# A three-stage decoder block on one core: the prologue's projections as three fp32r products, with context and inputs laid out ahead and loads on two queues

## The reference, cut to what matters

```python
# x: (2, 256, 128), ctx: (2, 512, 128), everything float32
x = x + attn(layernorm(x))          # 16 heads of 64, softmax over queries
x = x + xattn(layernorm(x), ctx)    # 16 heads of 8, 512 keys, mask over keys
x = x + moe(layernorm(x))           # 8 experts, 2 chosen, and a shared one; all 9 computed
# attn:  q, k, v = x_hat @ Wq + bq, x_hat @ Wk + bk, x_hat @ Wv + bv      (128 x 1024 each)
#        prob = softmax(k q^T / 8, axis=-2);  out = concat(prob @ v) @ Wo + bo
# xattn: q from x_hat, k and v from ctx (128 x 128 weights)
```

## Time and profile before

| | us |
|---|---|
| median of 3 runs | 220.93 |
| lowest and highest | 220.23, 222.34 |
| span of the profiled execution | 219.2 |
| TensorE busy | 202.3 (92%) |
| mean granted TensorE clock | 0.984 |

### The profile page before, as it was taken

One profiled execution on the slowest core, in us unless ns is written; L12 is line 12 of the kernel. 1 busy time (PEld: TensorE's weight loads), 2 busy tenths in 40 slices (PEclk: granted clock), 3 DMA queues, 4 the chain that ended last, 5 costly groups with the idle time before them and its releaser, 6 DMA issues.

```text
span 219.2 us, 4318 instructions
## 1 busy us (share of the span) xinstructions
PE 202.3 (92%) x1536; PEld 147.0 (67%) x1536; DVE 163.7 (75%) x424; ACT 126.4 (58%) x297; POOL 90.6 (41%) x136
## 2 busy tenths in 40 slices
PE   7599999799999799699796999999898999999993
PEld 7346466576767467456463665666565899999993
DVE  2628657878687799567999999998995685548843
ACT  2325436767575485536694989989696532372220
POOL 1989703764747466400899930000120002711332
PEclk9979999999999999979999999999999999999999
DMA  5960735999552003300601500000000000000000
GB/s 156 376 176 0 191 48 67 138 111 137 82 151 94 0 0 89 59 0 14 204 1 36 111 0 0 3 1 3 1 0 3 0 3 1 3 0 24 3 0 24
DMA packets 11740, 12.67 MB, mean 58 GB/s; under 512 B 848, under 2 KB 10064, under 8 KB 11648
## 3 DMA queue, kind: packets, MB, share of 16 engines
q1 hardware_dynamic: 11480, 12.20, 25.8%
q0 software_dynamic: 96, 0.20, 0.4%
q10 hardware_dynamic: 144, 0.01, 0.1%
HBM read 10.96 MB, written 1.44 MB: 57 GB/s over the span
## 4 chain that ended last, share of the span: by engine, by line
PE 74%; DVE 14%; issue 4%; ACT 3%; POOL 2%; DMA 2%; POOLq 0%; DVEq 0%
PE ps L830 12%; PE ps L792 8%; PE ps L721 7%; PE ps L736 7%; PE ps L851 7%; PE ps L629 7%; PE ps L708 6%; PE ps L770 6%; PE ps L752 5%; PE ps L641 4%; DVE q_t L1040 3%; DVE x_hat L915 2%; DMA x_in<-in_x 2%; PE ps L808 1%; DVE prob_t L1113 1%
## 5 line engine op out<-in xcount | busy, mean ns | idle before, releaser
L446 POOL TENSOR_TENSOR prob<-prob,rec 128x512 f32<-128x512 f32 x32 | 32.6, 1041 | 29.6 <-DVE rec L1095 29.6
L1040 DVE CUSTOM_DVE_ANT_0 q_t<-ps,mask_add 128x512 f32<-128x512 f32 x64 | 41.3, 682 | 2.1 <-PE ps L752 2.1
L531 ACT ACTIVATE prob<-ps,low 128x256 f32<-128x256 f32 x64 | 29.5, 475 | 18.4 <-DVE low L1030 18.4
L556 ACT ACTIVATE q_t<-q_t,low 128x512 f32<-128x512 f32 x44 | 29.4, 719 | 10.4 <-DVE low L1040 10.4
L386 POOL TENSOR_SCALAR var_eps<-mean_var 128x2 f32<-128x2 f32 (+1 forms) x5 | 1.1, 226 | 68.3 <-DVE mean_var L907 68.3
L792 PE MATMUL ps<-ident,q_t 128*128 128x128 f32 x176 | 23.4, 275 | 3.9 <-DVE place_o L1113 2.0
L792 PEld LDWEIGHTS ps<-ident,q_t 128*128 128x128 f32 x176 | 19.9, 141 | 9.2 <-issue 4.5
L1030 DVE TENSOR_REDUCE low<-ps 128x2 f32<-128x512 f32 x32 | 20.5, 683 | 6.3 <-PE ps L708 6.2
L1110 DVE COPY prob_t<-ps 128x512 f32<-128x512 f32 x32 | 20.6, 683 | 2.8 <-PE ps L736 2.8
L541 ACT ACTIVATE q_t<-ps 128x512 f32<-128x512 f32 x18 | 10.6, 598 | 21.0 <-PE ps L830 21.0
L752 PE MATMUL ps<-k_stack,q_stack 72*128 72x512 bf16 x64 | 19.3, 386 | 1.6 <-issue 1.6
(11 more groups left out here) (167 smaller groups left out, 422.3 us busy)
## 6 DMA issues: line engine op xcount, KB each, us to landing
k_stack<-k_dram SPq DMA_DIRECT2D x9, 256.0 KB
q_stack<-q_dram SPq DMA_DIRECT2D x6, 192.0 KB
wg<-in_L_ffn_w_gate SPq DMA_DIRECT2D x1, 1024.0 KB, 20.3
wu<-in_L_ffn_w_up SPq DMA_DIRECT2D x1, 1024.0 KB, 27.9
k_dram<-prob SPq DMA_DIRECT2D x1, 768.0 KB, 3.6
prob_t<-in_ctx SPq DMA_DIRECT2D x2, 256.0 KB, 4.0
w_in<-in_L_attn_Wq SPq DMA_DIRECT2D x1, 512.0 KB, 6.3
w_in<-in_L_attn_Wk SPq DMA_DIRECT2D x1, 512.0 KB, 7.1
```

The costliest lines, as they stand in the source:

```text
L446: nc.gpsimd.tensor_tensor(pr, pr, rec1[:, s % 2, r, :].unsqueeze(2).to_broadcast([P, C, S]), ALU.mult).then_inc(s_norm1, 1)
L531: e = nc.scalar.activation(prob1[:, s % 3, r, c * S:(c + 1) * S], ps[:, 2 * (s % 2) + r, c * S:(c + 1) * S], ACT.Exp, bias=low1[:, s % 2, ...
L556: nc.scalar.activation(prob2[n % 3][:, c, :], score2[n % 2][:, c, :], ACT.Exp, bias=low2[:, n % 2, c:c + 1], scale=-1.0).then_inc(s_exp2, 1)
L1040: nc.vector.tensor_tensor_reduce(out=score2[n % 2][:, c, :], in0=ps[:, 2 * (n % 2) + c, :], in1=mask_add[:, c, :], scale=1.0, scalar=3e38, ...
```

## The change

Five things change, all in the prologue:

1. `q` and `k` items are three fp32r products each instead of one fp32 product. The parts of the weights are made in halves of 512 columns: ACT rounds (`high_weights`), DVE subtracts (`low_weights`), both into the new tile `qk_parts`. The parts of `x_hat_t` (`xv_parts`) come straight from the PSUM bank of `x_t`: ACT rounds, DVE subtracts. POOL's split of `x_hat_t` and DVE's copy are gone.
2. The context comes transposed from the host, and x with a partition's four token rows side by side. The items `ctx_t` are gone, with their two ACT copies. The new order of items is `kx` 0, `kx` 1, `x_t`, `vx` 0, `vx` 1, then all `q` and `k`.
3. `wq1` and `wk1` are loaded in four halves (256 KB each) on ACT's queue, beside SP's.
4. POOL clears `v2` and fills `rank` before `reciprocal_std` instead of behind it.
5. The split of `k2_t` moves from DVE to POOL, in front of `x_bo`; its parts lie in another place of the tile `prob1`, so that ACT's wait for their way to DRAM (`d_kdram`) stands in front of the second head of `exp1(1)` instead of ahead of the whole loop.

```diff
 def items():
-    out = [("ctx_t", 0, "act"), ("ctx_t", 1, "act"), ("kx", 0, "act"), ("x_t", 0, "dve"), ("kx", 1, "act")]
+    out = [("kx", 0, "act"), ("kx", 1, "act"), ("x_t", 0, "dve"), ("vx", 0, "act"), ("vx", 1, "act")]
     for p in range(NP):
-        if p == 2:
-            out += [("vx", 0, "act"), ("vx", 1, "act")]
         out += [("q", p, "act"), ("k", p, "dve")]
...
+        qk_parts = retired("qk_parts", [P, 2, 2, H1 * HD1], F32R)
...
-            load(x_in[:, :, :], chunks(a["x"]), d_x)
-            for b in range(B):
-                load(ctx_in[:, b * KC:(b + 1) * KC, :], chunks(a["ctx_1024"])[:, b * KC:(b + 1) * KC, :], d_ctx[b])
+            load(x_in[:, :, :], a["x"], d_x)
+            load(ctx_t, a["ctx_1024"], d_ctx)
             load(wk2[:, :], a["L0_xattn_Wk"], d_wk2)
-            load(wq1, a["L0_attn_Wq"], d_wq1)
-            load(wk1, a["L0_attn_Wk"], d_wk1)
...
-            reciprocal_std(0, 0, NC_)
             nc.gpsimd.memset(v2[:, :, :, HD2 + 1:CW], 0.0)
...
+            reciprocal_std(0, 0, NC_)
...
             split(wv1, [wv1_parts[:, i, :] for i in range(2)]).then_inc(s_vparts, 1)
-            pool.wait_ge(s_ev["dve"], evacuated(index_of("x_t", 0))[1])
-            split(x_hat_t[:, :], [xv_parts[:, i, :] for i in range(2)]).then_inc(s_vparts, 1)
+            pool.wait_ge(s_ev["act"], evacuated(index_of("kx", 1))[1])
+            link(nc.gpsimd.tensor_copy(k2_parts[:, 0, :], k2_t))
+            link(nc.gpsimd.tensor_tensor(k2_rest, k2_t, k2_parts[:, 0, :], ALU.subtract))
+            link(nc.gpsimd.tensor_copy(k2_parts[:, 1, :], k2_rest))
+            nc.gpsimd.tensor_tensor(k2_parts[:, 2, :], k2_rest, k2_parts[:, 1, :], ALU.subtract).then_inc(s_kparts, 1)
...
+            for half in range(2):
+                for i, w in enumerate((wq1, wk1)):
+                    cols = slice(half * BANK, (half + 1) * BANK)
+                    act.dma_start(w[:, cols], a["L0_attn_W" + "qk"[i]][:, cols]).then_inc(d_qk[i][half], 16)
...
+            def high_weights(half):
+                cols = slice(half * BANK, (half + 1) * BANK)
+                for i, w in enumerate((wq1, wk1)):
+                    act.wait_ge(d_qk[i][half], 16)
+                    nc.scalar.copy(qk_parts[:, i, 0, cols], w[:, cols]).then_inc(s_whi, 1)
+
             for j, (kind, which, engine) in enumerate(ITEMS):
+                if (kind, which) == ("kx", 0):
+                    high_weights(0)
+                elif kind == "x_t":
+                    act.wait_ge(s_item, j + 1)
+                    nc.scalar.copy(xv_parts[:, 0, :], ps[:, j % 8, :]).then_inc(s_xhi, 1)
+                    high_weights(1)
                 if engine == "act":
                     evacuate(j, kind, which)
...
-            act.wait_ge(d_kdram, 16)
...
+                    if s == 1 and r == 1:
+                        act.wait_ge(d_kdram, 16)
...
-                    w = wq1 if kind == "q" else wk1
-                    last = mm(bank, w[:, which * P:(which + 1) * P], x_hat_t[:, :], start=True, stop=True)
+                    for part, (xi, wi) in enumerate(BIG_PARTS):
+                        last = mm(bank, qk_parts[:, i, wi, which * P:(which + 1) * P], xv_parts[:, xi, :],
+                                  start=part == 0, stop=part == len(BIG_PARTS) - 1)
...
+            def low_weights(half):
+                cols = slice(half * BANK, (half + 1) * BANK)
+                for i, w in enumerate((wq1, wk1)):
+                    dve.wait_ge(s_whi, 2 * half + i + 1)
+                    nc.vector.tensor_tensor(qk_parts[:, i, 1, cols], w[:, cols], qk_parts[:, i, 0, cols].bitcast(F32),
+                                            ALU.subtract).then_inc(s_qkparts, 1)
+
+            low_weights(0)
...
-                    ins = nc.vector.tensor_copy(x_hat_t[:, :], bank)
+                    dve.wait_ge(s_xhi, 1)
+                    ins = nc.vector.tensor_tensor(xv_parts[:, 1, :], bank, xv_parts[:, 0, :].bitcast(F32), ALU.subtract)
...
-                if (kind, which) == ("k", 1):
-                    dve.wait_ge(s_ev["act"], evacuated(index_of("kx", 1))[1])
-                    split(k2_t, k2_rest, k2_parts).then_inc(s_kparts, 1)
+                if kind == "x_t":
+                    low_weights(1)
...
+    laid["x"] = np.asarray(inputs["x"]).reshape(NC_, P, D).transpose(1, 0, 2)
+    laid["ctx_1024"] = np.asarray(inputs["ctx_1024"]).reshape(TK, D).T
```

More of the change, by code:

```diff
@@ L210, in build @@
         prob1_t_flat = prob1_t[:, :, :, :].rearrange("p a r n -> p (a r n)")
-        k2_parts = prob1_flat[:, 0:PARTS * TK // 2].bitcast(BF16).rearrange("p (j t) -> p j t", j=PARTS)
+        k2_parts = prob1_flat[:, PARTS * TK // 2:PARTS * TK].bitcast(BF16).rearrange("p (j t) -> p j t", j=PARTS)
         mask_in = prob1_t_flat[:, 0:C * SK].bitcast(mybir.dt.int32).rearrange("p (c k) -> p c k", c=C)
-        ctx_in = prob1_t_flat[:, C * SK:C * SK + B * KC * D].rearrange("p (c d) -> p c d", d=D)
         context = retired("context", [P, 3, TK])
@@ L280, in build @@
         d_x, d_wk2, d_wv2, d_wq2 = map(sem, ("d_x", "d_wk2", "d_wv2", "d_wq2"))
-        d_ctx = [sem(f"d_ctx{b}") for b in range(B)]
-        d_wq1, d_wk1, d_wv1, d_wo1 = map(sem, ("d_wq1", "d_wk1", "d_wv1", "d_wo1"))
+        d_ctx, d_wv1, d_wo1 = map(sem, ("d_ctx", "d_wv1", "d_wo1"))
+        d_qk = [[sem(f"d_w{n}1_{half}") for half in range(2)] for n in "qk"]
         d_bias, d_mask, d_bo, d_wo2, d_ffn, d_wd = map(sem, ("d_bias", "d_mask", "d_bo", "d_wo2", "d_ffn", "d_wd"))
@@ L293, in build @@
         s_ev = {"act": sem("s_ev_act"), "dve": sem("s_ev_dve")}
-        s_bq = sem("s_bq")
+        s_bq, s_whi, s_qkparts, s_xhi = map(sem, ("s_bq", "s_whi", "s_qkparts", "s_xhi"))
         s_var, s_rstd, s_xhat, s_xhat_ps, s_xhat_t = map(sem, ("s_var", "s_rstd", "s_xhat", "s_xhat_ps", "s_xhat_t"))
@@ L484, in evacuate @@
                 bank = ps[:, j % 8, :]
-                if kind == "ctx_t":
-                    ins = nc.scalar.copy(ctx_t[:, which * BANK:(which + 1) * BANK], bank)
-                elif kind == "kx":
+                if kind == "kx":
                     ins = nc.scalar.activation(k2_t[:, which * BANK:(which + 1) * BANK], bank, ACT.Identity,
@@ L603, in _ @@
                     pe.wait_ge(s_ev[engine], value)
[L604 to L608, removed]
+                if kind == "kx":
                     if which == 0:
                         pe.wait_ge(d_wk2, 16)
-                        pe.wait_ge(s_ev["act"], 2)
+                        pe.wait_ge(d_ctx, 16)
                     last = mm(bank, wk2[:, :], ctx_t[:, which * BANK:(which + 1) * BANK], start=True, stop=True)
@@ L623, in _ @@
                 else:
-                    if which == 0:
-                        pe.wait_ge(d_wq1 if kind == "q" else d_wk1, 16)
+                    i = "qk".index(kind)
+                    if which % (NP // 2) == 0:
+                        pe.wait_ge(s_qkparts, 2 * (which // (NP // 2)) + i + 1)
                     if kind == "q" and which == 0:
                         pe.wait_ge(s_ev["dve"], evacuated(index_of("x_t", 0))[1])
-                    w = wq1 if kind == "q" else wk1
-                    last = mm(bank, w[:, which * P:(which + 1) * P], x_hat_t[:, :], start=True, stop=True)
+                    for part, (xi, wi) in enumerate(BIG_PARTS):
+                        last = mm(bank, qk_parts[:, i, wi, which * P:(which + 1) * P], xv_parts[:, xi, :],
+                                  start=part == 0, stop=part == len(BIG_PARTS) - 1)
                 last.then_inc(s_item, 1)
@@ L705, in scores1 @@
                         pe.wait_ge(s_exp1, 2 * (s - 2) + r + 1)
+                    else:
+                        engine, value = evacuated(max(j for j in range(len(ITEMS)) if j % 8 == 2 * s + r))
+                        pe.wait_ge(s_ev[engine], value)
                     rows = slice(HD1 * r, HD1 * (r + 1))
@@ L800, in values_of_tokens @@
                         if i == 0:
-                            pe.wait_ge(s_vparts, 2)
+                            pe.wait_ge(s_vparts, 1)
                         engine, value = evacuated(max(j for j in range(len(ITEMS)) if j % 8 == V_BANKS[i]))
```

## The result

| | before | changed |
|---|---|---|
| median of the runs, us | 220.81 (4 runs) | 215.56 (4 runs) |
| lowest and highest | 220.23, 222.34 | 214.93, 215.91 |
| span of the profiled execution | 219.2 | 213.9 |
| mean granted TensorE clock | 0.984 | 0.992 |

The ratio is 0.975, with a 95% interval of 0.971 to 0.979: 5.3 us faster, against 216.0 us forecast.

The account below looks back on a forecast made before the run. Behind the prologue the last-ending chain was taken to run almost wholly through TensorE. Span 219.2 - 5.0 + 0.1 = 214.3 us, with the runs' median 1.7 above: 216.0 us; 8-in-10 range 212.9 to 218.5.

Parts of the forecast that it names:

- The first scores, 4.9 us sooner: End of the prologue on TensorE: the 48 q/k matmuls end at 24.4 us against 29.32, 4.9 to 5.0 us sooner.
- x_hat ready at 8.5: Prologue, DVE: with the clearing moved, x_hat takes 1.5 us at most and is ready at 8.5 instead of 10.55.
- Everything behind the first scores moves rigidly: After the prologue: waits are among engines and no load is due, so all later groups come 4.9 us earlier.
- The new small wait: Last item, k 7, lies in bank 4, which the second value bank needs: 0.1 us lost.
- The clearing: POOL's clearing of v2 moved early: x_hat comes 2 us sooner, but x_t waits for the key products, so nothing is gained.
- fp32r products, 2.8 us: q and k items on TensorE: three fp32r products instead of one fp32 save 16 x (0.86 - 0.685), 2.8 us.
- The second queue: Weights on ACT's queue share DMA engines with the context, which lands between 6.2 and 8.2 us; 7.2 taken.
- low for the key products: Start of TensorE's work: both key products run at the low clock level, 2 x 1.71 = 3.42 us, to 10.6.
- a granted clock of 0.50: Sign in the changed kernel's profile: the granted clock column reads 0.50 no later than 11 to 12 us.
- The rival with fast key products: Clock high for the key products, 2 x 0.86 us: q/k end at 22.2, 7.1 us sooner, time 213.9; chance 0.20.
- The second weak stretch: Clock's fall at 93 to 99 us: if it goes 214.4, if one more appears 217.6; no chance of its own.
- POOL as the bound: POOL's chain, 12.2 to 28.2 us, delays TensorE once 5.5 us longer; slowed throughout, the time is 227.6; chance 0.07.

Follow-up runs that it names:

- third job: One of three jobs of follow-up runs, each with the kernel before beside them; in this one the kernel before measured 219.9 us, the changed kernel run again 215.14.
- experiment 5: Changed kernel with 11 warm-up products instead of 8: 214.25 us; with value banks in order 7, 5, 6, 4 instead of 7, 4, 5, 6: 215.02; with both: 214.42.
- experiment 1: Changed kernel with POOL's clearing of v2 put back behind rstd: 215.78 us, ratio 0.977.
- experiment 2: Kernel before with only POOL's clearing of v2 moved ahead of rstd: 217.09 us beside 220.11, ratio 0.989.
- experiment 3: Changed kernel with one fp32 product per q and k item instead of three fp32r ones: 219.06 us, ratio 0.984.
- experiment 4: Changed kernel with the halves of wq1 and wk1 loaded on SP's queue behind x, context and wk2, none on ACT's: 215.46 us, ratio 0.971.
- experiment 6: Changed kernel with 20 unneeded additions put on POOL behind the additions to v2: 221.64 us, ratio 1.008.
- bank order: Changed kernel with the four self-attention value banks taken in order 7, 5, 6, 4 instead of 7, 4, 5, 6: 215.02 us, ratio 0.977.
- second profile: Changed kernel run once more with nothing changed, beside other kernels on one chip: 215.14 us, ratio 0.982, span 213.0.
- experiment 8: Changed kernel, all loads on SP's queue, wv2 before the weights, banks 7, 5, 6, 4, x_hat rounded earlier: 214.16 us; then parts in order of need: 212.81.
- Second job: Another of the three jobs of follow-up runs; the kernel before had a median of 220.1 us in it.

## Why the prediction was right

The time (216.0 against 215.56), the sign and the order of causes held. The forecast is a ratio of 0.978 to the kernel before. The first runs gave 0.975 and those of the third job 0.982, so it lies between the two, and how near the first came to it is in part luck. Point by point:

- *The first scores, 4.9 us sooner*: 4.7. The terms were off by more and cancelled. The context and `wk2` were there at 6.67 instead of 7.2 (-0.5). The key products took 3.78 us instead of 3.42 (+0.4). The transposes took 0.66 instead of 0.97, between the 0.44 of the high level and the 0.97 of the low one (-0.3). The value products came out exactly, 1.79. The 48 matmuls took 11.26 us, 0.235 each, instead of 10.96 (+0.3). That is above the 0.23 us that the prediction named as a sign of being wrong; the sign was set too tight.
- *x_hat ready at 8.5*: at 7.5. x landed at 3.56 instead of 4.0, the four instructions took 1.11 us instead of the 1.5 allowed, and POOL's DMA issues beside them held none up. The prediction also has `rstd` written at 5.83, where the earlier trace rows have its instruction start there and take 1.06.
- *Everything behind the first scores moves rigidly*: nearly. The lead is 4.7 us at the first scores, 5.1 and 6.5 later and 5.3 at the end. That the chain behind the prologue runs almost wholly through TensorE is too strong: from 103 to 118 us of the kernel before it runs almost wholly through DVE.
- *The new small wait*, 0.1 us: the group took 3.17 us against 2.74 without the stall, 0.4. I compared two durations and left out the semaphores on the way to DVE and back; experiment 5 gives the 0.4 back.
- *The clearing, of which "nothing is left"*: right, and shown by experiment 1, for slow key products. Experiment 2 shows that it does not hold where x_hat is what TensorE waits for. What I had not seen is how much of the whole gain it would bring alone, since I took the clock as a matter apart from x_hat.
- *fp32r products, 2.8 us*: 2.7 (experiment 3).
- *The second queue*: the row of 385 GB/s on one queue was read rightly, and experiment 4 confirms that the queue on ACT costs the context time, 1.6 us at `wk2`. I had taken the middle of the bounds, 1.0 above the early one.
- *The clock*: "low for the key products" was right for the first profile of the changed kernel; the sign that I named for it, a granted clock of 0.50, failed there, since that column read 1.00, and held in the second profile. The rival with fast key products was what an execution with the same prologue did (experiment 6). That the level follows from the gap is only half shown. Six profiles have the changed kernel's first products and its gap: in four (changed kernel, experiments 1 and 3, bank order) the key products took 3.7 to 3.8 us, in the changed kernel's second profile 2.77, in experiment 6 1.98. With 11 warm-up products they took 1.98 both times, and without a gap 3.1 once (experiment 4) and 2.0 to 2.1 twice (experiment 8). The high level is more frequent without the gap in these eleven profiles; the gap is not the only thing that decides, and what else does stays open.
- *The second weak stretch*: it moved from 93 to 113, as likely to win as to lose 1.6 us; it was a draw.
- *POOL as the bound*: not reached. POOL ended its additions at 26.6 instead of 28.2, because `wv1` landed 2 us earlier; its key split took 7.4 us against 7.1. Experiment 6 puts the threshold where it was reckoned and the price 2 us higher.

The 5.3 us between the medians then go, by the profiles: 2.7 by the products, 2.0 by the order of the prologue (work that no longer waits for x_hat, and less time at the low level, with 0.4 given back at the bank), 0.6 behind it. Only the 2.7, and the nothing of the clearing, are measured by taking the part back. The 2.0 are what is left: no run undoes the order of the items, the layouts made by the host or the key split's move to POOL by itself. How the times of many executions split between work and clock is open: at a granted clock of 0.992 the third job has the kernel before at 219.1 on average (8 executions) and the changed one at 215.1 (5), 4.0 apart where the medians of that job are 4.8 apart. The other 0.8 may be how often a weak stretch occurs: all 6 executions of the changed kernel have 0.992 or more, of the kernel before 10 of 17.

## What to carry to other kernels

Ask for each engine's wait what ends last there, and ask again after each part of a change: the same move was worth 2.4 us or more in one kernel and nothing in the other. Put the transfer that the first work waits for alone in front, on whatever queue, and write an engine's small preparations in the order in which their consumer needs them, so that a late transfer holds up only its own work. Where two kernels differ by less than a few us, compare the starts of the same groups and the averages of executions of equal granted clock, and trust neither from one execution.

## What the runs showed of the hardware

- The mean granted clock sorts the times in the main. Kernel before, third job: 217.7 to 217.8 us at 1.00 (2 executions), on average 219.1 at 0.992 (8), 221.0 at 0.984 (5) and 221.5 at 0.977 (2). Second job: 218.7 (2), 218.9 (8), 220.6 (6), 221.9 (4), and two at 0.985 with 222.5. A step of 0.008, about one weak stretch, goes with 0.2 to 1.9 us, and the same program has between none and three. The changed kernel's one execution at 1.00 in the third job, with 215.68, was slower than the average of its five at 0.992, 215.1.
- The same wait is or isn't followed by a weak stretch. In the kernel before the clock fell behind the 1.6 us ahead of 91 and not behind the 2.0 ahead of 118, in the changed kernel not behind the 1.3 ahead of 86 and did behind the 1.9 ahead of 112.
- The granted clock column can read 1.00 while TensorE works at its lower level at the start of a program: fp32 matmuls of 512 columns took 1061 ns at 6.7 to 9.4 us, 592 at least in the profile of the kernel before.
- Within a TensorE wait of 6.87 us the granted clock fell, and the work behind it ran at 0.50 until 43 us, so that 3.6 us of lateness cost 5.5 (experiment 6).
- The landing of the same 64 KB, behind the same transfers, lay between 6.62 and 7.21 us in six profiles of the same prologue.
